# A residual and a spiking membrane are added by identity products in PSUM instead of by VectorE

## What is computed

```python
x = x + _L0_conv_ref(_gn(x), ...)   # selective state-space block
x = x + _L1_conv_ref(_gn(x), W, b)  # linear layer, then spiking neurons over the images
```

```python
v = v + (x_t - v) / 2.0
s = (v - 1.0 >= 0)
v = v * (1.0 - s)
```

## Time and profile before

| | us |
|---|---|
| median of three runs | 4426.24 (4418.84 to 4433.01) |
| the profiled execution, its own time | 4415.12 |
| its span, first to last instruction | 4413.4 |
| DVE busy | 4047.4 (92%) |
| POOL busy | 3843.1 (87%) |
| PE busy | 3540.8 (80%) |
| ACT busy | 3411.3 (77%) |

### The profile page before, as it was taken

One profiled execution on the slowest core, in us unless ns is written; L12 is line 12 of the kernel. 1 busy time (PEld: TensorE's weight loads), 2 busy tenths in 40 slices (PEclk: granted clock), 3 DMA queues, 4 the chain that ended last, 5 costly groups with the idle time before them and its releaser, 6 DMA issues.

```text
span 4413.4 us, 64194 instructions
## 1 busy us (share of the span) xinstructions
PE 3540.8 (80%) x20244; PEld 2225.9 (50%) x20244; DVE 4047.4 (92%) x4017; ACT 3411.3 (77%) x5782; POOL 3843.1 (87%) x2518
## 2 busy tenths in 40 slices
PE   6787888888887788877888778887887788878876
PEld 3454555555555555545554555454554555445544
DVE  3999999999999999999999999999999999999996
ACT  4778787777877787777787777887787777878774
POOL 4999999889998899888999889988899888998894
PEclk8899999998999999999899999999999899999987
DMA  5233223322233223322232223222232223222310
GB/s 132 65 97 100 65 69 100 91 87 62 85 92 92 79 61 103 91 79 75 83 102 73 79 72 101 86 75 76 89 105 65 75 82 105 83 61 80 100 54 22
DMA packets 189295, 363.22 MB, mean 82 GB/s; under 512 B 27416, under 2 KB 164120, under 8 KB 188960
## 3 DMA queue, kind: packets, MB, share of 16 engines
q1 hardware_dynamic: 188960, 359.12, 27.7%
HBM read 289.84 MB, written 69.21 MB: 81 GB/s over the span
## 4 chain that ended last, share of the span: by engine, by line
DVE 26%; ACT 23%; PE 20%; issue 18%; POOL 12%; DVEq 0%; DMA 0%; POOLq 0%; ACTq 0%; SPq 0%
DVE st L1041 18%; POOL st L599 10%; PE ht L1190 8%; ACT decay L727 6%; DVE y L1017 3%; ACT L918 3%; ACT weighed L756 3%; PE work L1227 2%; ACT dt L799 2%; ACT L799 2%; PE work L1262 2%; PE work L1232 1%; PE work L1163 1%; ACT xb L878 1%; PE work L1222 1%
## 5 line engine op out<-in xcount | busy, mean ns | idle before, releaser
L1041 DVE TENSOR_TENSOR_SCAN st<-decay,st 128x1024 f32<-128x1024 f32 (+1 forms) x1536 | 2731.6, 1778 | 138.6 <-ACT decay L727 101.0
L599 POOL TENSOR_TENSOR st<-xc,bbc 128x1536 f32<-128x1536 f32 x768 | 2652.0, 3453 | 56.1 <-DMA bbc<-brow 46.9
L727 ACT ACTIVATE decay<-dt,neg_a 128x1024 f32<-128x1024 f32 (+1 forms) x1536 | 1356.8, 900 | 413.4 <-DVE st L1041 410.7
L1190 PE MATMUL ht<-ident,st 128*128 128x128 f32 x9216 | 1348.5, 297 | 337.1 <-DVE st L1041 299.9
L1190 PEld LDWEIGHTS ht<-ident,st 128*128 128x128 f32 x9216 | 1134.6, 153 | 648.8 <-DVE st L1041 465.1
L1017 DVE SCALAR_TENSOR_TENSOR y<-ht,ct,y 128x512 f32<-128x512 f32 x1536 | 1119.9, 729 | 89.8 <-PE ht L1190 89.4
L632 POOL TENSOR_TENSOR y<-y,weighed 128x512 f32<-128x512 f32 x672 | 854.4, 1271 | 340.3 <-ACT weighed L756 336.1
L756 ACT ACTIVATE weighed<-ht,ct 128x512 f32<-128x512 f32 x672 | 459.4, 684 | 274.1 <-PE ht L1190 271.7
L1227 PE MATMUL work<-xn,win 128*128 128x384 f32 x768 | 344.6, 594 | 136.7 <-DVE volt L997 103.2
L1163 PE MATMUL work<-tri,conv_w 96*32 96x384 f32 x4608 | 415.6, 493 | 5.2 <-issue 2.0
L1222 PE MATMUL work<-xn,win 128*128 128x480 f32 x768 | 359.9, 593 | 4.6 <-ACT xn L850 3.2
(11 more groups left out here) (109 smaller groups left out, 3173.2 us busy)
## 6 DMA issues: line engine op xcount, KB each, us to landing
bbc<-brow SPq DMA_DIRECT2D x192, 768.0 KB, 6.1
tri<-rows_of_xh SPq DMA_DIRECT2D x576, 200.0 KB, 3.9
rows_of_xh<-xhp SPq DMA_DIRECT2D x192, 250.0 KB, 2.4
out_dram<-ot SPq DMA_DIRECT2D x43, 384.0 KB, 4.2
xin<-in_x_dram SPq DMA_DIRECT2D x42, 384.0 KB, 3.4
st<-in_x_dram SPq DMA_DIRECT2D x6, 384.0 KB, 5.5
out_dram<-y SPq DMA_DIRECT2D x4, 384.0 KB, 2.6
brow<-xp SPq DMA_DIRECT2D x48, 24.0 KB, 1.5
```

The lines of the kernel that those rows point to most:

```text
L599: u = g.tensor_tensor(slot, xc[:, kq % 2, :, :], bbc[:, piece_slot(kq, p), n % PIECE, :].unsqueeze(1).to_broadcast([P, DC, T]), ALU.mult)
L727: a.activation(flat(decay[:, :, :])[:, lo:hi], flat(dt[:, (k + ahead) % 2, :, :])[:, lo:hi], ACT.Exp, scale=neg_a[:, n:n + 1]).then_inc(s_ ...
L1041: v.tensor_tensor_scan(state[:, lo:hi], flat(decay[:, :, :])[:, lo:hi], state[:, lo:hi], 0.0 if h == 0 else state[:, lo - 1:lo], ALU.mult, ...
L1190: last = t.transpose(ht[:, m, c * P:(c + 1) * P], st[:, j, c, m * P:(m + 1) * P], ident[:, :])
```

## The change

PE gets one more product in each group: the identity times the residual (in wo), or the identity times the old membrane (in l), ahead of the products that were there. The sum then stands in the PSUM bank when the group is done. DVE's charge goes; the bias is taken into the threshold (`fire_at` = 1 - `b1s` in the kernel's scaled units) and into ACT's copy of the membrane. DVE's residual instruction goes too: ACT empties wo with the bias `bo`. In the table wo0 moves from DVE's list to ACT's list of step 13, and wo1 from DVE's list of step 15 to ACT's list of step 14. The tail gets the same identity product.

```diff
-    13: ([], [(PRE2, "xh0")], [(POST, "wo0")]),
-    14: ([(PRE, "yi0")], [(PRE2, "xh1")], []),
-    15: ([(PRE, "yi1")], [], [(POST, "wo1")]),
+    13: ([], [(PRE2, "xh0"), (POST, "wo0")], []),
+    14: ([(PRE, "yi0")], [(PRE2, "xh1"), (POST, "wo1")], []),
+    15: ([(PRE, "yi1")], [], []),
...
+                    elif name[:2] == "wo":
+                        h = int(name[2:])
+                        xs = img[:, img_par(b, -1 if k == 0 else 0), h, (k - 1) % K * T:((k - 1) % K + 1) * T]
+                        bank_copy(name, xs, T, func=ACT.Identity, bias=bo[:, h:h + 1])
...
-                    a.activation(volt[:, h, kc * T:(kc + 1) * T], work[:, i, 0:T], ACT.Copy).then_inc(s_kept, 1)
+                    a.activation(volt[:, h, kc * T:(kc + 1) * T], work[:, i, 0:T], ACT.Identity,
+                                 bias=b1s[:, h:h + 1]).then_inc(s_kept, 1)
...
-                v.scalar_tensor_tensor(out=now, in0=now, scalar=b1s[:, h:h + 1], in1=volt[:, h, cols],
-                                       op0=ALU.add, op1=ALU.add).then_inc(s_volt, 1)
-                dve.wait_ge(s_volt, il + 1)
-                hold("dve", dve, b)
-                v.scalar_tensor_tensor(out=ob[:, h, :], in0=now, scalar=units[:, 1:2],
+                v.scalar_tensor_tensor(out=ob[:, h, :], in0=now, scalar=fire_at[:, h:h + 1],
...
-                        v.scalar_tensor_tensor(out=xs, in0=work[:, jw, 0:T], scalar=bo[:, h:h + 1],
-                                               in1=xs, op0=ALU.add, op1=ALU.add).then_inc(emptied[jw], 1)
...
+                            v.tensor_scalar(fire_at[:, :], b1s[:, :], -1.0, units[:, 1:2], ALU.mult,
+                                            ALU.add).then_inc(s_b1s, 1)
...
+                            t.matmul(work[:, i, 0:T], ident[:, :],
+                                     img[:, img_par(b, -1 if k == 0 else 0), h, (k - 1) % K * T:((k - 1) % K + 1) * T],
+                                     start=True, stop=False)
                             for c in range(DC):
                                 pe.wait_ge(s_yz, q0 * DC + c + 1)
                                 last = t.matmul(work[:, i, 0:T], wo[:, c, h * P:(h + 1) * P], zs[:, c, :],
-                                                start=c == 0, stop=c == DC - 1)
+                                                start=False, stop=c == DC - 1)
...
+                            t.matmul(work[:, i, 0:T], ident[:, :], volt[:, h, kc * T:(kc + 1) * T],
+                                     start=True, stop=False)
                             for hi in range(CH):
                                 last = t.matmul(work[:, i, 0:T], w1s[:, hi, h * P:(h + 1) * P],
                                                 img[:, img_par(b, -1), hi, kc * T:(kc + 1) * T],
-                                                start=hi == 0, stop=hi == CH - 1)
+                                                start=False, stop=hi == CH - 1)
```

More of the change, by code:

```diff
@@ L207, in vssm_lif_kernel @@
         b1s = sb("b1s", [P, CH])
+        fire_at = sb("fire_at", [P, CH])
         b1cs = sb("b1cs", [P, CH])
@@ L548, in _ @@
             g.memset(xhp[:, :, :, :], 0.0).then_inc(s_set_pool, 1)
-            g.memset(volt[:, :, :], 0.0)
+            g.memset(volt[:, :, :], 0.0).then_inc(s_set_pool, 1)
             def build_weights():
@@ L996, in reset @@
                 now = work[:, i, 0:T]
-                v.scalar_tensor_tensor(out=volt[:, h, cols], in0=now, scalar=units[:, 1:2], in1=volt[:, h, cols],
+                v.scalar_tensor_tensor(out=volt[:, h, cols], in0=now, scalar=fire_at[:, h:h + 1], in1=volt[:, h, cols],
                                        op0=ALU.is_lt, op1=ALU.mult).then_inc(emptied[i], 1)
@@ L1061, in iteration @@
                                 if a == BOTH_AT and s == a:
[L1062 removed]
+                                    fire(b, k, kc, 0)
                                 if a != BOTH_AT and s in (a, a + 1):
[L1064 removed]
+                                    fire(b, k, kc, s - a)
                         if s >= Y_LAG and main:
@@ L1127, in _ @@
                 cols = slice(kc * T, (kc + 1) * T)
-                now = ht[:, j % NHT, 0:T]
                 dve.wait_ge(s_end_l, j + 1)
-                v.scalar_tensor_tensor(out=now, in0=now, scalar=b1s[:, h:h + 1], in1=volt[:, h, cols],
-                                       op0=ALU.add, op1=ALU.add).then_inc(s_end_v, 1)
                 need(dve, s_end_t, 2 * (kc - 1))
-                dve.wait_ge(s_end_v, j + 1)
-                v.scalar_tensor_tensor(out=end_spikes(kc, h), in0=now, scalar=units[:, 1:2],
+                v.scalar_tensor_tensor(out=end_spikes(kc, h), in0=ht[:, j % NHT, 0:T], scalar=fire_at[:, h:h + 1],
                                        in1=img[:, img_par(B, -1), h, cols], op0=ALU.is_ge,
@@ L1159, in conv @@
                     pe.wait_ge(s_set_dve, 2)
-                    pe.wait_ge(s_set_pool, 5)
+                    pe.wait_ge(s_set_pool, 6)
                 for dx in range(TAPS):
@@ L1280, in iteration @@
                             pe.wait_ge(s_w1s, b)
+                            if b == 1:
+                                pe.wait_ge(s_set_pool, 5)
+                            else:
+                                await_emptied(pe, b - 1, k, name)
+                            t.matmul(work[:, i, 0:T], ident[:, :], volt[:, h, kc * T:(kc + 1) * T],
+                                     start=True, stop=False)
                             for hi in range(CH):
@@ L1317, in end_l1 @@
                 need(pe, s_end_f, j - NHT + 1)
+                t.matmul(ht[:, j % NHT, 0:T], ident[:, :], volt[:, h, kc * T:(kc + 1) * T], start=True, stop=False)
                 for hi in range(CH):
```

17 lines of the change are left out of this document (6 added, 11 removed).

## The result

The changed kernel takes 4475.21 us in the median of four runs (4461.68 to 4480.85) against 4426.87 for the kernel before (four runs): a ratio of 1.0106, 95% interval 1.0077 to 1.0135. It is 48 us slower. Its profiled execution took 4480.85 us, its span is 4478.9. The two profiled executions are extremes: that of the kernel before is the quickest on record, that of the changed kernel the slowest of its four, whose granted clocks run from 0.929 (4461.68) to 0.918 (4480.85). So differences between the profiles add up to 65.5 us and not to 48.

What follows compares the result with a forecast made beforehand. It took DVE as busiest (92%), but PE as full in steps 13 to 15. Terms 31.1 + 17.5 - 4 - 11.8 - 5.5 + 1.6 + 7.7 gave about +37 on 4426: 4463 us, range 4414 to 4492.

Steps and rivals of the forecast that it cites:

- the waits: Steps 13 to 15, chunk 2: DVE waits 0.75 us for state 13's transposes and 1.91 for state 14's.
- +31.1: Steps 13 to 15 of chunks 1 to 3, images 2 to 8: 21 windows lose 1.48 us each.
- +17.5: Steps 13 to 15 of chunks 4 and 5, and image 1's chunks 1 to 3: 19 windows lose 0.92 us each.
- Chunk 0: Its window from step 13 already took 17.06 us, because of PE's wait and clock, so no loss: 7 x 0.
- the threshold: Eight new instructions for the threshold at 0.2 us each: +1.6 us.
- POOL's term: DVE's scan waits for POOL, mostly in the chunk behind chunk 4, give back 0.5 us in eight images: -4.
- The spikes' term: Step 9's second half wins 21 x 0.56 = 11.8 us, step 2 wins 5.5, step 1 nothing.
- step 1 is like a first half: In step 1 the charges started close behind PE's products, so removing them wins 0.
- The tail: 13 identity products in series cost 8.4 us, less the last charge's 0.65: +7.7.
- that rival's number: Clock falls more often, in chunk 0 (4475 us) and perhaps also step 1 (4489); chance 0.18.
- DVE bounds the kernel everywhere: Rival: PE finds room for the products, 106 us won, 7.7 lost in the tail, 4328 us; chance 0.12.
- nothing measurable happens: Rival: the identity product is cheap (4426 us), or DVE's waits for ACT swallow about half the chunks' loss (4439); chance 0.18.

Runs made afterwards that it cites:

- e3: The changed kernel with PE's old order of the output halves, ACT still evicting both: 4423.58 us.
- e4: The changed kernel without wo's identity product, so the first block's residual is left out; new order, eviction and membrane part stay: 4428.32 us.
- e8: The kernel before with only identity transposes added in TensorE's idle stretches in steps 3, 7 and 10: 4356.88 us.
- e1: The kernel before with the output product's half alone (identity product ahead of wo, ACT's eviction with the bias, new table): 4488.48 us.
- e5: The changed kernel with 14 identity transposes in PE's idle stretch ahead of step 4's spike transposes (chunks 2 to 4, images 2 to 8): 4448.2 us.
- e6: e3 with the statistics of half 1 moved from the end of step 15 to step 0 of the next chunk: 4368.7 us.
- e7: e6 with identity transposes also in TensorE's idle stretches in steps 3, 7 and 10: 4314.27 us.
- e2: The kernel before with the membrane's half alone (identity product ahead of l, `fire_at`, ACT's membrane copy with the bias, the tail): 4407.15 us.

## Why the prediction was right

**The place and the size of the main loss were right.** The window of chunks 1 to 3 was to be 17.61 and is 17.72, that of the others 17.06 and is 17.13 or 17.03; the waits were to be 0.75 and 1.91 and are 0.75 and 1.80; the terms +31.1 and +17.5 are +33.4 and +15.1. The price of 0.645, taken from wo's own products, holds. e3 and e4 show that it takes both, the order and the product: without either, most of the loss in these windows is gone. The second term is 2.4 short because the last chunk has no such window and image 8's chunk 4 fell to 14.95.

**The total** was +37 and is +48 on the medians. By the estimate above, the windows of chunks 1 to 5 taken together (48.5 for 48.6) and the tail are right within half a microsecond; chunk 0 adds 2.9 that were put at nothing, and the start and steps 0 to 12 give back about 11, where the sum had 19.7.

**Chunk 0** came out right in images 2 to 8 (17.13 for 17.06), but by luck. The sum took 17.06 as the price of PE's wait and its clock. e8 keeps the kernel before's instructions and the same wait there, and in it the window alternates from image to image. Here are images 3 and 4, as windows and on PE's timeline:

```profile
1184.41:1200.54 16.13, 14.26 (x81) 10.39 (x80) 16.09 (x16) 10.87 (x20) 14.08 (x8) 1.00 0.60 186
1715.75:1732.79 17.04, 15.16 (x75) 11.23 (x73) 16.40 (x16) 10.46 (x20) 13.51 (x8) 0.90 0.52 168
```

```profile
1189.76 1.16 PE L1286 MATMUL work<-skip_diag,xc 128*128 128x128 f32 x8 [1.88 <-DVE img L1082]
1190.75 1.47 PE L1204 MATMUL ht<-ident,st 128*128 128x128 f32 x12
...
1721.10 1.40 PE L1286 MATMUL work<-skip_diag,xc 128*128 128x128 f32 x8 [1.88 <-DVE img L1082]
1722.29 2.77 PE L1204 MATMUL ht<-ident,st 128*128 128x128 f32 x12
```

So the wait costs nothing by itself, and half clock 0.91 us. In the changed kernel the new order costs 1.0 us there, as in the other chunks, and the clock, now 1.00, gives 0.9 back. In image 1 the window lost 2.3 us that I had not counted: 1.25 is the loss at full clock (e1 and e5), the rest comes with a clock of 0.90 in that window; e3, with the order back, loses nothing there.

**POOL's share and the threshold.** POOL's term, -4, failed. The scans' waits for POOL fell from 24.6 to 17.0 us, but that is no gain. DVE's timeline at step 4 of chunk 1 in image 3, in the kernel before and in the changed one:

```profile
1241.56 2.29 DVE L1041 TENSOR_TENSOR_SCAN st<-decay,st 128x1024 f32<-128x1024 f32 x1 [1.95 <-POOL st L606]
...
1256.08 1.55 DVE L1116 TENSOR_SCALAR fire_at<-b1s,units 128x2 f32<-128x2 f32 x1
1257.99 2.29 DVE L1041 TENSOR_TENSOR_SCAN st<-decay,st 128x1024 f32<-128x1024 f32 x1 [0.36 <-POOL st L606]
```

In seven images the threshold's instruction fills most of a wait that was there anyway. So it costs next to nothing (this step is 0.03 us longer on the mean, and 0.05 in e1, which has no such instruction), although its row is 1.55 us and not 0.2; the eighth, in the tail, takes 0.23, and why is open. Without the threshold, in e1, the waits for POOL are 28.8.

**The spikes' term failed in size.** At full clock (e5) step 9 of chunks 2 and 3 wins 0.57 each, the predicted 0.56; step 2 wins 0.38 where I had 0.26; and step 1, which I put at 0, wins as much: 6.01 against 6.39 at full clock before, 6.69 at half. So one step that failed is "step 1 is like a first half": the waits that it was read from stood, in step 1, only in steps at half clock (18 of 21); in the 3 at full clock the charge waited for nothing, and neither does the comparison in the changed kernel's 14. The other is that the sum has no term for the clock in steps 0 to 12. The gain is larger than predicted, and on the profiles the clock takes most of it back in step 4, +12.0, and in step 9, where 5 of 12 steps of chunks 2 and 3 in images 2 to 7 ran at 10.3 to 10.5 us. Step 9 of chunk 1 never won: 9.06 against 8.95, with half-clock time in it on both sides.

**The tail** was to lose 7.7 and lost 8.2. The start came 2.5 us later; over the eight other kernels it varied from 0.4 to 6.0, also where nothing there had changed, so I do not put this down to the change.

**The rivals.** The clock did fall in new places, but in steps 4 and 9, not in chunk 0: 4475 came out for that rival's number, not for its place. e5 tells them apart: with the half clock gone from step 4, the change still costs 24 us. On the profiles these are 31: windows 50, tail and start 12, less 31 in steps 0 to 12. That DVE bounds the kernel everywhere is refuted for this order and nearly true for another: in e6 the windows of chunks 1 to 3 come to within 0.75 us of DVE's busy time. That nothing measurable happens is refuted by the ratio's interval. The rule by occupancy alone (the Trainium skill, "Perfetto Trace Analysis", Identifying the Most-Contended Engine) took 90 us off the busiest engine here and the time rose by 48. For the other page cited, the Trainium skill, "TensorE: Matmul & The Clock Gate", HAM oscillation, e5, e7 and e8 agree: filling TensorE's gaps gave 27, 54 and 67 us. The windows of e8 above add that the same gap of 1.88 us is followed by full clock in one image and by half clock in the next.

Why the stretch at half clock moves from step 1 to step 4 as the spikes get shorter is not settled. The idle stretch ahead of step 4 was 2.03 us in the kernel before and is 2.31 in the same step after; e3, with no half-clock time in step 1, has it in 17 of the 21 steps 4. No run changes that stretch's length alone.

## What to carry to other kernels

When an edit moves work from the busiest engine to another, walk the receiving engine's order in the stretch itself: what counts is which consumer's data now comes later, not whose mean share is lower. The same products and evictions cost 16 us in one order of the queue (e2 to e3) and 68 in another (e2 to the changed kernel), so try the edit with the old order before judging it. And look at the granted clock step by step on both sides: a gain in one step may be given back in a later one where an idle stretch is followed by half clock. Before calling a term right because its total fits, look whether two errors cancel in it, as the order and the clock did in chunk 0.

## What the runs showed of the hardware

Transposes whose result nobody reads, put into idle stretches of about 2 to 5 us, raised the granted clock over the span from 0.922 to 0.952 in the kernel before (e8) and from 0.927 to 0.955 in the best version (e6 to e7), and made them 67 and 54 us faster. I had expected the clock to matter in chunk 0 and step 1 alone. Step durations at the two levels stand apart: in the kernel before and the changed one step 4 of chunks 2 to 4 takes 5.20 or 5.21 us at full clock and 6.1 to 6.7 with half-clock time in it; in other kernels the slow ones begin at 5.8. Sorting a step's durations over the images shows such a split at a glance, but the clock has to be read beside it: five steps 11 of the changed kernel hold half-clock time and take 5.33, as short as any.
